# Plain attention on one core: the weighting matmuls between the two score tiles of a period, one period later

## The chip, the cores and the metric

The kernel runs on one core of a Trainium2 chip. The metric is the device time of one execution in microseconds (us), from the first to the last instruction. The engines are TensorE (PE in the profile; PEld is its weight load), VectorE (DVE), ScalarE (ACT), GpSimd (POOL) and SyncE (SP), which issues most DMAs. Each works through its own queue in order, and semaphores order the queues against each other.

## The reference

The input is x with 4 batches of 1024 tokens and 128 dims. Four blocks follow each other, each added to x: a causal attention with rotary keys, a mixture of 8 experts, a plain attention, and the experts again. The change lies in the plain attention:

```python
q = (x @ Wq.T).reshape(N, S, H, hd).transpose(0, 2, 1, 3)     # H = 16 heads of hd = 8
k = (x @ Wk.T)...
v = (x @ Wv.T)...
energy = jnp.einsum('nhqd,nhkd->nhqk', q, k)
attn = jax.nn.softmax(energy / jnp.sqrt(jnp.float32(hd)), axis=3)
out = jnp.einsum('nhql,nhld->nhqd', attn, v)
```

## The kernel before

`attend_plain` (line 1002) works in 16 head stacks (`STEPS`): one batch and 4 heads each. A stack has two halves of 512 query columns, and a half has 16 periods (`NP`). So there are 512 periods t (`LAST`), and all five engines write out the same loop `for t in range(-LEAD, LAST + 8)`.

The kernel computes the scores twice. First, 26 periods ahead (`LEAD`), with queries in rows: `score(w, r)` (line 1081), w = t + 26, fills one half of a double bank `wide[w % 2]` with 128 queries x 512 keys of one head. Two such, with r = 1 and r = 0, make one tile of 1024 columns, and VectorE takes the maximum of each half in one reduction (line 1174). Both `score` matmuls of w go into the bank that reduction w - 2 has read: in front of `score(w, 1)` TensorE waits for it (`s_sf`), and the reduction waits for both scores (`s_s`). The maxima of a half are split by GpSimd in three bf16 parts, turned by a matmul (line 1156), copied by ScalarE (line 1220) and brought by four DMAs into extra rows of the query stack.

Then, in period t, with keys in rows: `t_score(u)` (line 1074) for the units u = 2t and 2t + 1 fills `bank[u % 2]` with 128 keys x 512 queries, from which the maximum is already subtracted through the extra rows. ScalarE takes the exponential into a slot of the ring `pT` (line 1208). In front of `t_score(u)` TensorE waits until exponential u - 2 has read the bank. Four units, one for each head, make a quad; `weigh(quad, half)` (line 1088) multiplies the four exponentials by the values `vst`, for one half of the columns. It issues four matmuls, in the trace eight of 256 columns, into the accumulating bank 2 + J of the half J. One such half of a quad is done in each period.

`t_score(u)` with even u uses the array's rows from 0 and stands beside `score(w, 1)` in the rows from 64; `t_score(u + 1)` with `score(w, 0)` is the other way about. These are called the first and the second pair below. TensorE's order in one period before the change is: first pair, second pair, `weigh` of period t - 2, at the end of a half the transposes, and in one period of 16 the turning of the maxima.

At the end of a half, in periods given by `ends_half(t, later)`: ScalarE copies the weighted sums out (`o_sb`, line 1214), TensorE transposes them in four matmuls (line 1149), VectorE divides by the sum of the exponentials (lines 1188 and 1191), and every second time GpSimd writes the values of the stack after next (line 1247). `late_step` and `step_at` give periods in which steps of the next stage's routing are worked in: a few in stacks 9 to 14, and one in two of three periods behind `BEGIN`, where no scores are left to compute (26 periods).

Of the kernel before, what the change touches and what calls it, by code (L numbers as in the profile page):

```python
# [20 lines left out]
GH = 4  # L21
# [22 lines left out]
def mk_program(nc, x_in, w_kv_down, w_k_up, w_v_up, w_q, w_q_rope, w_k_rope, w_o, wq_b, wk_b, wv_b,  # L44
               router_w, w1, b1, w2, b2, cos2, sin2, out):
    ctx = ExitStack()
    with ctx:
# [954 lines left out]
        def attend_plain(stacks, results, s_parts):  # L1002
# [2 lines left out]
            LAST = 2 * STEPS * NP  # L1005
            HEADS = (0, 2, 1, 3)
            KROW = MROW + 3
            NPB = 2 * GH
            s_row = [sem(f"max_rows{i}") for i in range(2)]
            s_s, s_sf = sem("score_pair", False), sem("score_max", False)  # L1010
            s_mall, s_mch, s_m3, s_mt, s_m = sem("max_whole"), sem("split_chain"), sem("max_split"), sem("max_turned"), sem("max_kept")
# [25 lines left out]
            def half_of(t):  # L1037
                return t // NP
# [28 lines left out]
            def late_step(t, place):  # L1067

                return t >= BEGIN and (t - BEGIN) % 3 == place

            with nc.Block() as block:
                @block.tensor
                def _(e):
                    def t_score(u):
                        s, J, kc, j = unit(u)
                        r, jj, at = j // 2, j % 2, s % NBUF
                        e.matmul(bank[u % 2][:, :], k_st[at][64 * r:64 * r + KROW, jj, kc * P:(kc + 1) * P],  # L1077
                                 q_st[at][64 * r:64 * r + KROW, jj, J * HALF:(J + 1) * HALF],
                                 start=True, stop=True, tile_position=(64 * r, 0)).then_inc(s_st, 1)

                    def score(w, r):
                        s, G, pair, c, kh = score_at(w)
                        at, q0 = s % NBUF, (G % 2) * HALF + c * P
                        e.matmul(wide[w % 2][:, r * HALF:(r + 1) * HALF], q_st[at][64 * r:64 * r + MROW, pair, q0:q0 + P],  # L1084
                                 k_st[at][64 * r:64 * r + MROW, pair, kh * HALF:(kh + 1) * HALF],
                                 start=True, stop=True, tile_position=(64 * r, 0)).then_inc(s_s, 1)

                    def weigh(quad, half):
                        for i in range(GH):
                            u = quad * GH + i  # L1090
                            s, J, kc, j = unit(u)
                            qs = slice(half * HALF // 2, (half + 1) * HALF // 2)
                            ins = e.matmul(bank[2 + J][32 * j:32 * (j + 1), qs], vst[s % 2][:, kc, j, :], pT[:, u % NPB, qs],  # L1093
                                           start=(kc == 0 and half == 0), stop=(kc == NC - 1 and half == 1),
                                           tile_position=(0, 32 * j), skip_group_check=True)
                            if half:
                                ins.then_inc(s_pv, 1)

                    steps = routed.tensor(e)
                    for t in range(-LEAD, LAST + 8):  # L1100
                        w, u = t + LEAD, 2 * t
                        tiles, scores = 0 <= t < LAST, w < LAST
                        if t - 3 in step_at:
                            s = (t - 3) // (2 * NP)
                            e.wait_ge(s_y, PRIME + 2 * s)
                            e.wait_ge(s_m, PRIME + 2 * s + 2)
                            next(steps)
                        if t == BEGIN:
                            e.wait_ge(s_sf, LAST)
                        if late_step(t, 0):  # L1110
                            next(steps, None)
                        if tiles:
                            if t % (2 * NP) == 0:
                                e.wait_ge(stacks.s_in[unit(u)[0] % NBUF], stacks.loaded(unit(u)[0]))
                            if t % NP == 0:
                                e.wait_ge(s_row[half_of(t) % 2], PRIME + (half_of(t) // 2 + 1) * 64)
                            if u >= 2:
                                e.wait_ge(s_p, PRIME + u - 1)
                            t_score(u)
                        if scores:  # L1120
                            if w % (2 * NP) == 0:
                                e.wait_ge(stacks.s_in[score_at(w)[0] % NBUF], stacks.loaded(score_at(w)[0]))
                            if w >= 2:
                                e.wait_ge(s_sf, w - 1)
                            score(w, 1)
                        if late_step(t, 1):
                            next(steps, None)
                        if tiles:
                            if u >= 2:
                                e.wait_ge(s_p, PRIME + u)  # L1130
                            t_score(u + 1)
                        if scores:
                            score(w, 0)
                        if 0 <= t - 2 < LAST:
                            quad, half = divmod(t - 2, 2)
                            if t == 2:
                                e.wait_ge(s_vz, PRIME + 4)
                            if (t - 2) % (2 * NP) == 0:
                                e.wait_ge(s_vs, PRIME + half_of(t - 2) // 2 + 1)
                            if (t - 2) % (2 * NP) == NP and half_of(t - 2) // 2 in LENT:  # L1140
                                e.wait_ge(s_lent, half_of(t - 2) // 2 - LENT[0] + 1)
                            if half == 0:
                                e.wait_ge(s_p, PRIME + (quad + 1) * GH)
                            weigh(quad, half)
                        H = ends_half(t, 3)
                        if H is not None:
                            e.wait_ge(s_oev, PRIME + H + 1)
                            for c in range(CPH):
                                ins = e.transpose(bank[2 + H % 2][:, c * P:(c + 1) * P], o_sb[:, c * P:(c + 1) * P], ident[:, :])
                            ins.then_inc(s_ot, 1)  # L1150
                        G = turns_max(t)
                        if G is not None:
                            e.wait_ge(s_m3, PRIME + G + 1)
                            if G >= 2:
                                e.wait_ge(s_y, PRIME + G - 1)
                            e.matmul(bank[2 + G % 2][0:GH * 3 * CPH, 0:P], mx3[G % 2][:, :, :, :].rearrange("p j i c -> p (j i c)"),
                                     identb[:, :], start=True, stop=True).then_inc(s_mt, 1)
                    drain(steps)

                @block.vector  # L1160
                def _(e):
                    steps = routed.vector(e)
                    for t in range(-LEAD, LAST + 8):
# [7 lines left out]
                        if w < LAST:  # L1171
# [4 lines left out]
                            if w % NP == NP - 1:  # L1176
                                e.wait_ge(s_sf, w + 1)
                                if G >= 2:
                                    e.wait_ge(s_m3, PRIME + G - 1)
                                e.tensor_tensor(mxw[G % 2][:, :, :], mx[G % 2][:, 0, :, :], mx[G % 2][:, 1, :, :],  # L1180
                                                ALU.max).then_inc(s_mall, 1)
                        H = ends_half(t, 4)
                        if H is not None:
                            e.wait_ge(s_ot, PRIME + H + 1)
                            if H >= 1:
# [13 lines left out]
                @block.scalar  # L1199
                def _(e):  # L1200
                    steps = routed.scalar(e)
                    for t in range(-LEAD, LAST + 8):
                        if 0 <= t < LAST:
                            for u in (2 * t, 2 * t + 1):
                                e.wait_ge(s_st, PRIME + u + 1)
                                if u >= NPB:
                                    e.wait_ge(s_pv, PRIME + (u // GH - 1) * GH)
                                e.activation(pT[:, u % NPB, :], bank[u % 2][:, :], ACT.Exp, scale=scale).then_inc(s_p, 1)  # L1208
                        H = ends_half(t, 1)
                        if H is not None:  # L1210
                            e.wait_ge(s_pv, PRIME + (H + 1) * NP * 2)
                            if H >= 1:
                                e.wait_ge(s_ot, PRIME + H)
                            e.activation(o_sb[:, :], bank[2 + H % 2][:, :], ACT.Copy).then_inc(s_oev, 1)
                        G = turns_max(t)
                        if G is not None:
                            e.wait_ge(s_mt, PRIME + G + 1)
                            if G >= 2:
                                e.wait_ge(s_row[G % 2], PRIME + G // 2 * 64)
                            e.activation(nmp[G % 2][:, :], bank[2 + G % 2][0:GH * 3 * CPH, 0:P], ACT.Copy).then_inc(s_m, 1)  # L1220
                        if t - 3 in step_at:
                            next(steps)

                @block.gpsimd
                def _(e):
# [10 lines left out]
                    for t in range(-LEAD, LAST + 8):  # L1236
# [3 lines left out]
                            next(sums, None)  # L1240
                        if t in (19 * NP + 10, 19 * NP + 12):
                            next(normed)
                        H = ends_half(t, 3)
                        if H is not None and H % 2 and H // 2 + 2 < STEPS:
                            s = H // 2 + 2
                            e.wait_ge(s_pv, PRIME + (H + 1) * NP * 2)
# [883 lines left out]
```

## Time and profile before

| | before |
| --- | --- |
| median of 3 runs (lowest, highest) | 2027.02 us (2025.97, 2036.19) |
| profiled execution, own time | 2027.0 us |
| its span | 2027.0 us |
| PE busy | 1782.4 us, 88% |
| DVE busy | 1410.1 us, 70% |
| ACT busy | 1161.5 us, 57% |
| POOL busy | 581.1 us, 29% |

The plain attention of the change takes the time from about 1034 us (first `score`) to 1763 us. Busy shares are means over all stages; the share of a stage is read from windows. A line of a timeline gives start, duration, engine, line, operation, and how many instructions it merges. The duration of a matmul is from its start until its result is there; matmuls overlap, so distances between starts say what TensorE needs.

### The profile page before, as it was taken

What the parts mean: (1) busy time and instruction counts of PE and PEld (TensorE: products, weight loads), DVE (VectorE), ACT (ScalarE), POOL (GpSimd) and SP (SyncE); (2) the same over time, 40 slices, a digit from 0 to 9 for tenths busy, and PEclk for the clock granted to TensorE, in tenths of its full rate; (3) what the DMA queues carried; (4) which work ended last, traced back from release to release, by engine and by line L of the source; (5) the groups of instructions that cost most, each with busy time, mean ns of one, the idle gap of its engine ahead of it and who ended that gap; (6) DMA issues with size and microseconds to landing.
All of it is one profiled execution on the core that took longest, in us unless ns stands there. A gap on an engine that the chain in (4) does not pass through costs nothing. (4 is left out here: it accounts for less than half of the span.)

```text
span 2027.0 us, 40740 instructions
## 1 busy us (share of the span) xinstructions
PE 1782.4 (88%) x15061; PEld 903.7 (45%) x15061; DVE 1410.1 (70%) x3172; ACT 1161.5 (57%) x2314; POOL 581.1 (29%) x817
## 2 busy tenths in 40 slices
PE   5699999999999968799659999999999999777895
PEld 2356666565655545475312222222233332255563
DVE  6676666667788455532669999999899998557431
ACT  3336666666655632232328888888888887332231
POOL 2312122121122146676330000002310000157774
PEclk9779999999999978888769999999999998579798
DMA  5642744553541053232220000000000000062324
GB/s 158 160 81 51 125 84 72 101 90 61 104 81 17 23 143 60 41 53 35 88 110 14 21 17 18 23 27 18 17 18 20 28 5 22 14 168 37 60 38 83
DMA packets 108006, 120.95 MB, mean 60 GB/s; under 512 B 14361, under 2 KB 72961, under 8 KB 107809
## 3 DMA queue, kind: packets, MB, share of 16 engines
q1 hardware_dynamic: 83616, 100.97, 21.1%
q0 software_dynamic: 24192, 17.38, 6.1%
q8 instruction: 120, 1.97, 0.4%
q14 instruction: 78, 0.63, 0.1%
HBM read 81.71 MB, written 35.65 MB: 58 GB/s over the span
## 5 line engine op out<-in xcount | busy, mean ns | idle before, releaser
L1174 DVE TENSOR_REDUCE mx<-wide 128x2 f32<-128x1024 f32 x512 | 604.6, 1220 | 55.2 <-PE wide L1084 42.9
L1208 ACT ACTIVATE pT<-bank 128x512 f32<-128x512 f32 x1024 | 556.8, 596 | 110.9 <-PE bank L1077 102.7
L870 ACT ACTIVATE pT<-bank 128x512 f32<-128x512 f32 (+3 forms) x768 | 350.5, 490 | 248.3 <-PE bank L723 230.0
L1077 PE MATMUL bank<-q_st,k_st 51*128 51x512 bf16 x1024 | 360.4, 397 | 21.0 <-ACT pT L1208 5.2
L1084 PE MATMUL wide<-k_st,q_st 48*128 48x512 bf16 x1024 | 352.6, 399 | 23.6 <-DVE mx L1174 13.9
L1093 PE MATMUL bank<-pT,vst 128*32 128x256 f32 x4096 | 340.2, 405 | 1.8 <-DVEq L1168 1.8
L837 DVE TENSOR_REDUCE mx<-wide 128x1 f32<-128x640 f32 (+3 forms) x256 | 257.2, 1021 | 102.8 <-PE wide L733 97.8
L733 PE MATMUL wide<-k_st,q_st 120*128 120x512 f32 (+3 forms) x768 | 311.1, 417 | 3.5 <-DVE mx L837 1.7
L723 PE MATMUL bank<-q_st,k_st 122*128 122x512 f32 (+3 forms) x768 | 297.8, 392 | 5.5 <-ACT pT L870 3.4
L1793 POOL DMA_INDIRECT acc_rows<-yg,idx x128 | 201.9, 1577 | 105.0 <-DVE yg L2060 71.8
L1077 PEld LDWEIGHTS bank<-q_st,k_st 51*128 51x128 bf16 x1024 | 90.3, 93 | 311.5 <-ACT pT L1208 268.0
L910 POOL TENSOR_SCALAR_AFFINE_SELECT pT<-pT 128x512 f32<-128x512 f32 x128 | 81.0, 633 | 363.8 <-ACT pT L870 363.7
L723 PEld LDWEIGHTS bank<-q_st,k_st 122*128 122x128 f32 x768 | 143.9, 189 | 92.3 <-ACT pT L870 41.6
L1881 PE MATMUL wide<-xgT,w1b 128*128 128x512 f32 x256 | 158.9, 764 | 12.1 <-ACT xgT L1944 4.4
L748 PE MATMUL bank<-pT,vst 128*32 128x256 f32 (+3 forms) x3072 | 164.6, 332 | 1.1 <-POOL pT L910 0.6
L733 PEld LDWEIGHTS wide<-k_st,q_st 120*128 120x128 f32 x768 | 158.9, 208 | 10.7 <-DVE mx L837 9.7
L1093 PEld LDWEIGHTS bank<-pT,vst 128*32 128x32 f32 x4096 | 82.0, 109 | 137.7 <-issue 135.2
L1950 ACT ACTIVATE hT<-wide,b1t 128x512 f32<-128x512 f32 x128 | 87.3, 687 | 95.5 <-PE wide L1881 88.0
L1781 POOL DMA_INDIRECT xg<-xn_rows,idx x128 | 124.7, 974 | 56.6 <-issue 41.8
L731 PE MATMUL wide<-mask_qk,identb 128*128 128x128 bf16 x512 | 121.9, 238 | 16.7 <-PEq L371 11.7
L1255 POOL CAST mx<-mxw 128x16 bf16<-128x16 f32 x32 | 6.3, 196 | 435.2 <-DVE mxw L1180 431.9
L1944 ACT ACTIVATE xgT<-bank 128x512 f32<-128x512 f32 x32 | 19.1, 597 | 163.7 <-PE bank L1869 122.3
(328 smaller groups left out, 2041.0 us busy)
## 6 DMA issues: line engine op xcount, KB each, us to landing
q_st<-rope_split SPq DMA_DIRECT2D x60, 256.0 KB
k_st<-rope_split SPq DMA_DIRECT2D x60, 256.0 KB
qk_split<-parts SPq DMA_DIRECT2D x8, 1024.0 KB, 6.6
q_st<-qk_split SPq DMA_DIRECT2D x96, 64.0 KB
k_st<-qk_split SPq DMA_DIRECT2D x96, 64.0 KB
qk_parts<-parts SPq DMA_DIRECT2D x8, 768.0 KB, 4.6
xn_rows<-xn SPq DMA_DIRECT2D x8, 512.0 KB, 4.0
w1b<-in_L_ffn_w SPq DMA_DIRECT2D x16, 256.0 KB, 5.2
```

Source lines behind the costliest of these rows:

```text
L723: e.matmul(bank[u % 2][:, q0:HALF], k_st[at][0:KROW, j, kc * P:(kc + 1) * P], q_st[at][0:KROW, J, j, q0:HALF], start=True, stop=True).then ...
L733: return e.matmul(wide[w % 2][:, col:col + width], q_st[at][0:KS, G % 2, j, c * P:(c + 1) * P], k_st[at][0:KS, j, kh * HALF:kh * HALF + wi ...
L748: ins = e.matmul(bank[2 + J][32 * j:32 * (j + 1), qs], vst[s % 2][:, kc, j, :], pT[:, u % NPB, qs], start=(kc == 0 and half == 0), stop=(k ...
L837: ins = e.tensor_reduce(mx[G % 2][:, at:at + 1], wide[w % 2][:, 0:HALF + right], AX.X, ALU.max)
L870: e.activation(pT[:, u % NPB, q0:HALF], bank[u % 2][:, q0:HALF], ACT.Exp, scale=scale).then_inc(s_p, 1)
L1077: e.matmul(bank[u % 2][:, :], k_st[at][64 * r:64 * r + KROW, jj, kc * P:(kc + 1) * P], q_st[at][64 * r:64 * r + KROW, jj, J * HALF:(J + 1) ...
L1084: e.matmul(wide[w % 2][:, r * HALF:(r + 1) * HALF], q_st[at][64 * r:64 * r + MROW, pair, q0:q0 + P], k_st[at][64 * r:64 * r + MROW, pair, ...
L1093: ins = e.matmul(bank[2 + J][32 * j:32 * (j + 1), qs], vst[s % 2][:, kc, j, :], pT[:, u % NPB, qs], start=(kc == 0 and half == 0), stop=(k ...
L1174: e.tensor_reduce(mx[G % 2][:, kh, pair:GH:2, c], wide[w % 2][:, :].rearrange("p (r k) -> p r k", r=2), AX.X, ALU.max).then_inc(s_sf, 1)
L1208: e.activation(pT[:, u % NPB, :], bank[u % 2][:, :], ACT.Exp, scale=scale).then_inc(s_p, 1)
L1793: e.indirect_dma_start(acc_dram[n // NE], bass.IndirectOffsetOnAxis(ap=idx[n % 4][:, m:m + 1], axis=0), yg[n % 2][:, m, :], None, compute_ ...
L1881: e.matmul(tile_bank[(tiles_to(n) + k) % 2], w1b[:, ex, k * P:(k + 1) * P], xgT[n % 2][:, :], start=True, stop=True).then_inc(s_h, 1)
```

## The change

`weigh` moves from behind the second pair to between the first and the second pair of a period, and works on period t - 3 in place of t - 2, with all of its waits. The steps that follow the end of a half (copy, transposes, division, values) come one period later with it. The ring of exponentials grows from 8 to 12 slots, and the wait in front of an exponential is written for a ring of any multiple of 4.

```diff
--- before.py
+++ after.py
@@ -1005,7 +1005,7 @@
             LAST = 2 * STEPS * NP
             HEADS = (0, 2, 1, 3)
             KROW = MROW + 3
-            NPB = 2 * GH
+            NPB = 12
             s_row = [sem(f"max_rows{i}") for i in range(2)]
             s_s, s_sf = sem("score_pair", False), sem("score_max", False)
             s_mall, s_mch, s_m3, s_mt, s_m = sem("max_whole"), sem("split_chain"), sem("max_split"), sem("max_turned"), sem("max_kept")
@@ -1123,6 +1123,17 @@
                             if w >= 2:
                                 e.wait_ge(s_sf, w - 1)
                             score(w, 1)
+                        if 0 <= t - 3 < LAST:
+                            quad, half = divmod(t - 3, 2)
+                            if t == 3:
+                                e.wait_ge(s_vz, PRIME + 4)
+                            if (t - 3) % (2 * NP) == 0:
+                                e.wait_ge(s_vs, PRIME + half_of(t - 3) // 2 + 1)
+                            if (t - 3) % (2 * NP) == NP and half_of(t - 3) // 2 in LENT:
+                                e.wait_ge(s_lent, half_of(t - 3) // 2 - LENT[0] + 1)
+                            if half == 0:
+                                e.wait_ge(s_p, PRIME + (quad + 1) * GH)
+                            weigh(quad, half)
                         if late_step(t, 1):
                             next(steps, None)
                         if tiles:
@@ -1131,18 +1142,7 @@
                             t_score(u + 1)
                         if scores:
                             score(w, 0)
-                        if 0 <= t - 2 < LAST:
-                            quad, half = divmod(t - 2, 2)
-                            if t == 2:
-                                e.wait_ge(s_vz, PRIME + 4)
-                            if (t - 2) % (2 * NP) == 0:
-                                e.wait_ge(s_vs, PRIME + half_of(t - 2) // 2 + 1)
-                            if (t - 2) % (2 * NP) == NP and half_of(t - 2) // 2 in LENT:
-                                e.wait_ge(s_lent, half_of(t - 2) // 2 - LENT[0] + 1)
-                            if half == 0:
-                                e.wait_ge(s_p, PRIME + (quad + 1) * GH)
-                            weigh(quad, half)
-                        H = ends_half(t, 3)
+                        H = ends_half(t, 4)
                         if H is not None:
                             e.wait_ge(s_oev, PRIME + H + 1)
                             for c in range(CPH):
@@ -1179,7 +1179,7 @@
                                     e.wait_ge(s_m3, PRIME + G - 1)
                                 e.tensor_tensor(mxw[G % 2][:, :, :], mx[G % 2][:, 0, :, :], mx[G % 2][:, 1, :, :],
                                                 ALU.max).then_inc(s_mall, 1)
-                        H = ends_half(t, 4)
+                        H = ends_half(t, 5)
                         if H is not None:
                             e.wait_ge(s_ot, PRIME + H + 1)
                             if H >= 1:
@@ -1204,9 +1204,9 @@
                             for u in (2 * t, 2 * t + 1):
                                 e.wait_ge(s_st, PRIME + u + 1)
                                 if u >= NPB:
-                                    e.wait_ge(s_pv, PRIME + (u // GH - 1) * GH)
+                                    e.wait_ge(s_pv, PRIME + ((u - NPB) // GH + 1) * GH)
                                 e.activation(pT[:, u % NPB, :], bank[u % 2][:, :], ACT.Exp, scale=scale).then_inc(s_p, 1)
-                        H = ends_half(t, 1)
+                        H = ends_half(t, 2)
                         if H is not None:
                             e.wait_ge(s_pv, PRIME + (H + 1) * NP * 2)
                             if H >= 1:
@@ -1240,7 +1240,7 @@
                             next(sums, None)
                         if t in (19 * NP + 10, 19 * NP + 12):
                             next(normed)
-                        H = ends_half(t, 3)
+                        H = ends_half(t, 4)
                         if H is not None and H % 2 and H // 2 + 2 < STEPS:
                             s = H // 2 + 2
                             e.wait_ge(s_pv, PRIME + (H + 1) * NP * 2)
```

## Rows read from the trace of the kernel before

**Rows 1.** Page, costliest groups: busy us, mean ns of one | idle before, releaser.

```profile
L1174 DVE TENSOR_REDUCE mx<-wide 128x2 f32<-128x1024 f32 x512 | 604.6, 1220 | 55.2 <-PE wide L1084 42.9
L1208 ACT ACTIVATE pT<-bank 128x512 f32<-128x512 f32 x1024 | 556.8, 596 | 110.9 <-PE bank L1077 102.7
...
L1077 PE MATMUL bank<-q_st,k_st 51*128 51x512 bf16 x1024 | 360.4, 397 | 21.0 <-ACT pT L1208 5.2
...
L1093 PE MATMUL bank<-pT,vst 128*32 128x256 f32 x4096 | 340.2, 405 | 1.8 <-DVEq L1168 1.8
```

**Rows 2.** Waits from 1080 to 1450 us: total us, times, longest.

```profile
PEld bank L1077 <- ACT pT L1208: 151.8, 380, 0.7
...
ACT pT L1208 <- PE bank L1077: 39.1, 108, 0.9
DVE mx L1174 <- PE wide L1084: 15.3, 36, 0.5
```

**Rows 3.** Timeline of ScalarE: start us, us, engine, line.

```profile
1186.31 2.19 ACT L1208 ACTIVATE pT<-bank 128x512 f32<-128x512 f32 x4 [0.26 <-PE bank L1077]
1188.77 2.19 ACT L1208 ACTIVATE pT<-bank 128x512 f32<-128x512 f32 x4 [0.26 <-PE bank L1077]
```

**Rows 4.** Timeline of TensorE, two periods.

```profile
1188.34 0.39 PE L1077 MATMUL bank<-q_st,k_st 51*128 51x512 bf16 x1
...
1188.57 0.38 PE L1077 MATMUL bank<-q_st,k_st 51*128 51x512 bf16 x1
...
1188.88 0.64 PE L1093 MATMUL bank<-pT,vst 128*32 128x256 f32 x8
...
1189.45 0.39 PE L1077 MATMUL bank<-q_st,k_st 51*128 51x512 bf16 x1
...
1189.91 0.39 PE L1077 MATMUL bank<-q_st,k_st 51*128 51x512 bf16 x1
...
1190.22 0.64 PE L1093 MATMUL bank<-pT,vst 128*32 128x256 f32 x8
...
1190.80 0.39 PE L1077 MATMUL bank<-q_st,k_st 51*128 51x512 bf16 x1
```

**Rows 5.** Timeline while only scores run (before period 0).

```profile
1039.92 2.34 DVE L1174 TENSOR_REDUCE mx<-wide 128x2 f32<-128x1024 f32 x2
...
1041.19 0.11 PEld L1084 LDWEIGHTS wide<-k_st,q_st 48*128 48x128 bf16 x2 [1.03 <-DVE mx L1174]
```

**Rows 6.** Timeline at the end of a half.

```profile
1192.64 0.39 PE L1084 MATMUL wide<-k_st,q_st 48*128 48x512 bf16 x1
...
1193.10 1.23 DVE L1174 TENSOR_REDUCE mx<-wide 128x2 f32<-128x1024 f32 x1 [0.38 <-PE wide L1084]
...
1193.53 0.66 PE L1149 MATMUL bank<-ident,o_sb 128*128 128x128 f32 x4
1194.11 0.09 PEld L1077 LDWEIGHTS bank<-q_st,k_st 51*128 51x128 bf16 x1 [0.17 <-issue]
...
1194.80 1.23 DVE L1174 TENSOR_REDUCE mx<-wide 128x2 f32<-128x1024 f32 x1 [0.47 <-PE wide L1084]
...
1196.43 1.22 DVE L1174 TENSOR_REDUCE mx<-wide 128x2 f32<-128x1024 f32 x1
```

**Rows 7.** Timeline of ScalarE, copies at ends of halves.

```profile
1128.99 0.60 ACT L1214 ACTIVATE o_sb<-bank 128x512 f32<-128x512 f32 x1
...
1201.76 0.27 ACT L1220 ACTIVATE nmp<-bank 48x128 bf16<-48x128 f32 x1
...
1232.36 0.60 ACT L1214 ACTIVATE o_sb<-bank 128x512 f32<-128x512 f32 x1
```

**Rows 8.** Windows: busy us (instructions) of each engine, PEclk, DMA share, GB/s.

```profile
1300.00:1450.00 150.00, 145.18 (x1434) 43.92 (x1432) 140.65 (x139) 131.42 (x248) 36.13 (x80) 1.00 0.07 23
...
1706.00:1760.00 54.00, 49.93 (x302) 13.01 (x301) 30.00 (x193) 29.84 (x54) 0.83 (x4) 0.53 0.07 21
```

**Rows 9.** Timeline behind the last tile of scores.

```profile
1757.95 0.58 PE L1676 MATMUL wide<-tail,same_rowf 128*128 128x1 f32 x2 [1.07 <-DVE tail L1622]
```

## What was predicted, before the change was run

> **What bounds the kernel now.** I read the page first, then its costliest groups, then the waits of one quiet stretch, then the timeline of single periods. The groups show the change's stage: 512 periods, each with two exponentials of 596 ns on ScalarE, one maximum reduction of 1220 ns on VectorE, two pairs of score matmuls and eight weighting matmuls on TensorE [rows 1]. No engine alone fills a period. In 370 us VectorE waited 15.3 us for the score pairs, ScalarE 39.1 us for TensorE, and TensorE 151.8 us (380 waits) for ScalarE, as prefetched weight loads see it [rows 2]. So the bound is a ring between TensorE and ScalarE, and the timeline shows it: ScalarE does four exponentials in 2.19 us, then waits 0.26 us for a score, again and again, 2.46 us from one group to the next, which is 1.23 us a period [rows 3].
>
> The two periods behind that [rows 4]: pair 1188.34, pair 1188.57, weighting 1188.88; pair 1189.45, pair 1189.91 (0.46 later, held by an exponential), weighting 1190.22, pair 1190.80. I read off the distances between starts that TensorE needs by itself: pair to pair 0.22 (0.23), pair to weighting 0.32, weighting to pair 0.57. With nothing to wait for a period would be 0.22 + 0.32 + 0.57 = 1.11 us. The late exponential every second period makes it 1.23.
>
> VectorE has the third loop. Reduction w and the scores of w + 2 share a double bank, so `score(w+2, 1)` waits for reduction w, and reduction w + 2 waits for `score(w+2, 0)`. Its links: from the start of a reduction to the matmul pair it releases, 1039.92 to 1041.19, 1.27 us [rows 5]; from the start of the second score to its reduction, 1192.64 to 1193.10, 0.46 us [rows 6]. Before the change the two scores lie 0.22 apart, so the loop needs 1.27 + 0.22 + 0.46 = 1.95 us for two periods that take 2.46: half a microsecond of play, and it does not bind.
>
> **The change, part by part.**
>
> Moving the weighting between the pairs. It removes and adds no TensorE instruction. The distances stay too: pair, weighting, pair, next pair is 0.32 + 0.57 + 0.22 = 1.11 us. For the bank that an exponential frees nothing changes either: score tiles of the exponentials were 0.22 and 0.89 apart by turns, now 0.89 and 0.22. I therefore expect no gain for ScalarE. But `score(w, 1)` stands ahead of the eight matmuls and `score(w, 0)` behind them: queued behind the first score's wait for VectorE are the weighting, the next tile of scores and then the very score that this reduction needs. The VectorE loop becomes 1.27 + 0.89 + 0.46 = 2.62 us for two periods, 1.31 us each. That exceeds 1.23: the cover of half a microsecond is gone and VectorE's loop sets the time. Sixteen periods (one half of a head stack): 16 x 1.31 = 20.96 us.
>
> Work at the ends of halves. Before, a whole half takes 20.67 us: the o_sb copies at 1128.99 and 1232.36 are five halves apart [rows 7]. Sixteen times 1.23 is 19.7, so 1.0 us per half is now the work at its ends. In the new order each such item eats the play beside the loop first. VectorE's two normalising operations push one reduction from 1.12 behind the last (2.34 for two, less 1.22 for one) [rows 5] to 1.63 (1194.80 to 1196.43) [rows 6]: 0.51, less the play of 1.31 - 1.12 = 0.19, leaves 0.32. The four transposes now follow the second pair: 0.32 to them and 0.58 from them to the next pair (1193.53 to 1194.11) [rows 6] in place of 0.22, so 0.68 added, less the play of 0.20 (1.31 - 1.11), leaves 0.48. On ScalarE the second exponential of a period now starts late (0.89 + 0.43 after the first pair; 0.43 is from 1188.34 to 1188.77 [rows 3, 4]), ends its slot of 0.53 at 1.85, and the next, ended at 2.45, is needed at 2.62: play 0.17. The 0.60 us copy (a slot of 0.5) [rows 7] leaves 0.32, the 0.27 us copy of the turned maxima (a slot of 0.3) 0.13. All four: 1.25 us. Each falls on one of two interleaved chains, which absorb a little of each other's delays, so I take 1.2 with 0 and 1.4 as ends. A half: 20.96 + 1.2 = 22.2 us, 1.5 more than now.
>
> How often. Scores run 26 periods ahead, so score pairs and tiles run together in 486 of 512 periods: 30.4 halves x 1.5 = 45.6 us. The 26 periods without scores have no VectorE loop. There TensorE runs at 0.50 to 0.53 of full clock and is 49.9 of 54 us busy, with the next stage's routing steps in between [rows 8]; the order of work inside them costs the same either way, between -2 and +2 us. The first half's stretch at low clock is TensorE's own work and counts in the same bound.
>
> A TensorE rule. Pair to pair takes 0.22 us but pair to weighting 0.32 [rows 4], so changing kind of matmul costs about 0.10. A period has two such changes before and after. At a half's end the transposes and the turning of the maxima stood between weighting and pair and now stand between two pairs, one more change for each. The Trainium skill, TensorEngine Tiling (Array Packing), Key Properties, says that changing the tiling mode drains TensorE; by it the edit costs two more drains per half, which the trace prices at about 0.1 us each, some 6 us in all if nothing covered them. By a view that modes are free, they would be nothing. The sums above hold the transposes' own from rows.
>
> One period later, and the tail. Weighting half a quad at t - 3 leaves one more weighting block behind the last score tile. At half the clock a block takes up to twice its 0.57 us. But the routing matmul there waits 1.07 us for VectorE [rows 9], and the additional block falls ahead of it: between 0 and +1 us, I take 0. The o_sb copy, transposes, division and reload of v each move by one period with it; the wait of ScalarE for the last weighting gets shorter, as the weighting is now done mid-period. SP's queue is left where it is. The values for the next stack are needed a period later and are made a period later. From -1 to +1, taken as 0.
>
> The ring of 12. An exponential waits for the weighting of the quad it overwrites. No row of waits has ScalarE on the weighting line for it before [rows 2], and now exponentials of period t overwrite what was weighted by period t - 2. Price 0. With the old ring of 8 the first exponential of every second period would wait for the weighting in the middle of its own period, at 0.32 + 0.57 behind the pair instead of 0.43 [rows 4]; the longer ring is what the move needs. Nothing is gained by it alone.
>
> Sum: 2027.0 + 45.6 = 2072.6 us. The profiled execution's own time is its span, 2027.0, against a median of 2027.02, so nothing is converted.
>
> **Rivals.**
>
> Faster by even spacing. The weighting between the tiles could feed ScalarE evenly and close its 0.26 us gap. For: ScalarE's slot pair is 1.06 us, TensorE's floor 1.11 [rows 3, 4]. Against: the VectorE loop must come under 2.46 us, and it needs scores within 0.73 of each other, where the rows give 0.89. It decides where the weighting between row-tiled pairs costs 0.16 us less than beside them. With a period at 1.18 it gives 16 x 0.05 = 0.8 us a half, 2027 - 24 = 2003 us. Chance 0.05.
>
> No difference. The loop rises only to about 2.5 us, or half-end work disappears wholly in the play: 20.96 against 20.67 is +0.3 a half, +9 us, 2036; with the loop at 2.5, -5 to +5. Chance 0.10.
>
> The clock falls. TensorE's real waiting grows from 0.12 to 0.20 us in each period. In the quiet stretch the granted clock is 1.00 with TensorE 145 of 150 us busy, in the tail 0.53 [rows 8]. The Trainium skill, TensorE: Matmul & The Clock Gate, A second HAM failure mode, tells of a kernel that cycles PSUM banks and idles briefly between matmul groups until its clock oscillates. As a mechanism here: all of TensorE's 1.11 us doubles at half the clock, so a period takes 2.2 us in place of 1.39. If a tenth of the 627 us ran so, some 37 us come on top (63 x (2.2 - 1.39) / 1.39): about 2110. The trace speaks against it, since gaps of ScalarE's kind never lowered the clock there. Chance 0.04.
>
> The change isn't what it says: the order could be moved while waits make it idle. Only the ring is such a part, and it is priced at nothing already.
>
> **How the numbers follow.** Forecast 2073, chance 0.81, own range 2050 to 2090: the low end has loop links 0.04 shorter (16 x 0.02 x 30.4 = 10 us) and half of the half-end work covered, the high end 1.4 of it and links 0.04 longer. With no difference 0.10, faster 0.05, clock 0.04 this fills 1. For eight in ten 2045 to 2092. A change under 0.5% (10 us) is what a measurement of this kernel can't tell. From the cases: faster 0.05, same 0.10, slower 0.85.
>
> **What would show it.** Right: VectorE waiting for the score matmuls in nearly every period, its reductions 1.31 us apart in quiet stretches; weight loads of L1084 released by the reduction, which the rows of waits do not have now; the o_sb copies 22.2 us apart; ScalarE waiting on L1077 as often; weighting starts 0.32 behind a pair. Wrong: the second score under 0.8 us behind the first, reductions 1.23 apart, or a granted clock under 0.95 between 1100 and 1450 us.

## The result: 2.7% slower, by VectorE's loop

| | before | after |
| --- | --- | --- |
| median | 2026.7 us (4 runs) | 2084.6 us (2081.0 to 2089.7, 4 runs) |
| ratio of after to before | | 1.0273, interval 1.024 to 1.0307 |
| profiled execution, own time | 2027.0 us | 2081.0 us |
| its span | 2027.0 us | 2079.1 us |
| plain attention, first reduction to first division of the last half | 1034.3 to 1762.4 us | 1030.1 to 1810.05 us |

The prediction was 2073 us. Placed beside the kernel before once more, on what by its times is another chip (2005.8 us for the kernel before), the kernel after gave 1.0248 (1.0213 to 1.0283). In the profiles the attention takes 51.8 us more and the span 52.1, so the change sits where it was expected. The stages that it doesn't touch moved a little and cancel: the attention starts 4.2 us earlier, and what follows it takes 4.45 us more. The distance between the medians is 4 us larger than between the two profiled executions (54). The slowest of the four executions after (2089.7 us) has the lowest mean granted clock, 0.912 against 0.917 to 0.919; beyond that I can't place these 4 us.

The page's groups after the change. Read the last column: the idle time before an operation, and who ended it.

```profile
L1174 DVE TENSOR_REDUCE mx<-wide 128x2 f32<-128x1024 f32 x512 | 606.6, 1221 | 105.2 <-PE wide L1084 104.7
L1208 ACT ACTIVATE pT<-bank 128x512 f32<-128x512 f32 x1024 | 568.3, 596 | 166.0 <-PE bank L1077 157.2
...
L1077 PE MATMUL bank<-q_st,k_st 51*128 51x512 bf16 x1024 | 363.0, 399 | 26.8 <-ACT pT L1208 17.8
L1093 PE MATMUL bank<-pT,vst 128*32 128x256 f32 x4096 | 342.4, 408 | 0.0
```

The work is what it was [rows 1]: the same counts and the same durations. Waiting has grown on VectorE (55 to 105 us) and on ScalarE (111 to 166 us). The waits from 1080 to 1450 us, in the order total, times, longest:

```profile
PEld bank L1077 <- ACT pT L1208: 138.1, 331, 0.8
...
ACT pT L1208 <- PE bank L1077: 65.4, 168, 0.8
...
DVE mx L1174 <- PE wide L1084: 46.1, 133, 0.6
...
PEld wide L1084 <- DVE mx L1174: 12.6, 16, 0.8
```

VectorE waits for its score matmuls 133 times instead of 36 [rows 2], about once in two periods, and a new row has come: score matmuls held by the reduction. Its 16 waits are one a half, 0.79 us each, where VectorE does other work; in quiet periods the hold is too short for this row. There it shows inside the first pair, whose two matmuls start 0.18 us apart (1188.08 and 1188.26 below) and were 0.01 apart before. Now one turn of the loop, from the timeline of VectorE and TensorE:

```profile
1186.97 2.36 DVE L1174 TENSOR_REDUCE mx<-wide 128x2 f32<-128x1024 f32 x2 [0.27 <-PE wide L1084]
...
1188.08 0.39 PE L1077 MATMUL bank<-q_st,k_st 51*128 51x512 bf16 x1
...
1188.26 0.39 PE L1084 MATMUL wide<-k_st,q_st 48*128 48x512 bf16 x1
...
1188.57 0.64 PE L1093 MATMUL bank<-pT,vst 128*32 128x256 f32 x8
...
1189.15 0.39 PE L1084 MATMUL wide<-k_st,q_st 48*128 48x512 bf16 x1
...
1189.60 2.36 DVE L1174 TENSOR_REDUCE mx<-wide 128x2 f32<-128x1024 f32 x2 [0.27 <-PE wide L1084]
```

A reduction starts at 1186.97. The first score into its bank starts at 1188.26, 1.29 later, when the reduction is over. The weighting comes next, and the second score 0.89 behind the first. The next reduction into the bank starts 0.45 behind that, at 1189.60. Sum 2.63 us for two periods; predicted were 1.27 + 0.89 + 0.46 = 2.62. Reductions come in close pairs and then wait 0.27, since two banks make two interleaved chains.

ScalarE's copies at the ends of halves, two in a row:

```profile
1130.89 0.59 ACT L1214 ACTIVATE o_sb<-bank 128x512 f32<-128x512 f32 x1
...
1153.24 0.59 ACT L1214 ACTIVATE o_sb<-bank 128x512 f32<-128x512 f32 x1
```

A quiet half takes 22.35 us, against 20.67 [rows 7]. Last the end of a half:

```profile
1197.45 0.60 ACT L1208 ACTIVATE pT<-bank 128x512 f32<-128x512 f32 x1 [0.41 <-PE bank L1077]
...
1197.95 0.59 ACT L1214 ACTIVATE o_sb<-bank 128x512 f32<-128x512 f32 x1
...
1199.09 0.39 PE L1077 MATMUL bank<-q_st,k_st 51*128 51x512 bf16 x1 [0.53 <-ACT pT L1208]
...
1199.98 0.39 PE L1084 MATMUL wide<-k_st,q_st 48*128 48x512 bf16 x1
1200.30 0.66 PE L1149 MATMUL bank<-ident,o_sb 128*128 128x128 f32 x4
...
1200.43 1.23 DVE L1174 TENSOR_REDUCE mx<-wide 128x2 f32<-128x1024 f32 x1 [0.58 <-PE wide L1084]
1200.88 0.39 PE L1077 MATMUL bank<-q_st,k_st 51*128 51x512 bf16 x1
...
1202.23 1.23 DVE L1174 TENSOR_REDUCE mx<-wide 128x2 f32<-128x1024 f32 x1 [0.57 <-PE wide L1084]
```

The copy holds exponentials up, and they hold the pair at 1199.09 by 0.53. The transposes stand 0.32 behind the second pair and 0.58 ahead of the next, as the terms of the sum had it, and the two reductions behind wait 0.58 and 0.57 instead of 0.27. What VectorE does next was not all in the sum:

```profile
1203.49 0.17 DVE L1180 TENSOR_TENSOR mxw<-mx 128x16 f32<-128x16 f32 x1
1203.59 0.25 DVE L1188 RECIPROCAL rsum<-bank 128x16 f32<-128x16 f32 x1
1203.87 0.29 DVE L1191 TENSOR_TENSOR v_all<-bank,rsum 128x128 f32<-128x128 f32 x1
1204.08 2.35 DVE L1174 TENSOR_REDUCE mx<-wide 128x2 f32<-128x1024 f32 x2
1206.69 2.36 DVE L1174 TENSOR_REDUCE mx<-wide 128x2 f32<-128x1024 f32 x2 [0.27 <-PE wide L1084]
```

The two normalising operations come one period later than before, and there they meet L1180, which merges the maxima of the half. The reduction starts 1.85 us behind the last one, 0.73 above VectorE's 1.12. From 1206.69 on five turns of 2.63 us follow to the end of the half. The windows of a quiet stretch and of the 54 us behind the last early scores:

```profile
1300.00:1450.00 150.00, 142.19 (x1328) 47.27 (x1327) 130.56 (x129) 121.89 (x229) 21.11 (x52) 1.00 0.05 18
1752.80:1806.80 54.00, 51.23 (x302) 13.42 (x305) 30.90 (x195) 30.43 (x55) 0.83 (x4) 0.55 0.07 21
```

Against [rows 8]: 129 VectorE instructions instead of 139 in 150 us, at full clock both times, and behind the last scores the same 302 matmuls in the same 54 us. From the last reduction to the first division of the last half it is 56.8 us before and 57.2 after.

### The profile page after: what moved, and what is told of

Read it like the earlier page. It is cut to its first block and busy times, and to the rows that moved or that the text cites. A ratio compares the mean times of both kernels' runs of the same rounds, so it can differ in the third digit from the quotient of the medians.

```text
span 2079.1 us, 40736 instructions
## 1 busy us (share of the span) xinstructions
PE 1822.9 (88%) x15061; PEld 932.6 (45%) x15061; DVE 1414.4 (68%) x3172; ACT 1163.2 (56%) x2314; POOL 580.5 (28%) x817
## 3 DMA queue, kind: packets, MB, share of 16 engines
q1 hardware_dynamic: 83616, 100.97, 20.7%
## 5 line engine op out<-in xcount | busy, mean ns | idle before, releaser
L1174 DVE TENSOR_REDUCE mx<-wide 128x2 f32<-128x1024 f32 x512 | 606.6, 1221 | 105.2 <-PE wide L1084 104.7
L1208 ACT ACTIVATE pT<-bank 128x512 f32<-128x512 f32 x1024 | 568.3, 596 | 166.0 <-PE bank L1077 157.2
L1084 PE MATMUL wide<-k_st,q_st 48*128 48x512 bf16 x1024 | 365.8, 402 | 33.4 <-DVE mx L1174 23.7
L1077 PE MATMUL bank<-q_st,k_st 51*128 51x512 bf16 x1024 | 363.0, 399 | 26.8 <-ACT pT L1208 17.8
L1077 PEld LDWEIGHTS bank<-q_st,k_st 51*128 51x128 bf16 x1024 | 89.0, 93 | 313.7 <-ACT pT L1208 262.9
L1084 PEld LDWEIGHTS wide<-k_st,q_st 48*128 48x128 bf16 x1024 | 92.0, 93 | 83.3 <-DVE mx L1174 49.9
```

The lines of the kernel that those rows point to most:

```text
L1174: e.tensor_reduce(mx[G % 2][:, kh, pair:GH:2, c], wide[w % 2][:, :].rearrange("p (r k) -> p r k", r=2), AX.X, ALU.max).then_inc(s_sf, 1)
```

## The experiments

Each was timed beside the kernel before on the same chip, but they were spread over three chips: e1 to e4 on one (median of the kernel before 2005.1 us), e5 to e8 on a second (2000.7), e9 and the second timing of after on a third (2005.8). So ratios are compared, and the length of a quiet half, which repeats to about 0.01 us within a profile. Whole times scatter more than the halves, by up to 1.3% between executions of the same kernel, and e6 was timed only twice.

```
kernel                                   ratio to before (interval)    quiet half, us
before                                   1                             20.67
after                                    1.0248 (1.0213 to 1.0283)     22.35
e1 weighting behind the pairs, t - 3     0.9979 (0.9946 to 1.0011)     20.53
e2 after, scores side by side            1.0066 (1.0035 to 1.0098)     20.98
e3 before, scores parted                 1.0217 (1.0151 to 1.0283)     22.01
e4 after, reductions an eighth shorter   1.0119 (1.0037 to 1.0201)     21.47
e5 after, reductions of half the keys    1.0066 (1.0044 to 1.0087)     20.95
e6 after, ring of 8                      1.0642 (1.0606 to 1.0678)     24.52
e7 e2, transposes behind the weighting   1.0050 (1.0031 to 1.0068)     21.12
e8 e1, transposes a period later         0.9962 (0.9941 to 0.9983)     20.51
e9 before, transposes a period later     0.9957 (0.9936 to 0.9977)     20.45
```

(The half of before is from the chip of the result; the half of after is 22.35 there and in the second timing.)

**Is it the later period or the longer ring?** e1 is the kernel after with one block moved back:

```diff
                         if scores:
                             ...
                             score(w, 1)
-                        if 0 <= t - 3 < LAST:
-                            ...
-                            weigh(quad, half)
 ...
                             score(w, 0)
+                        if 0 <= t - 3 < LAST:
+                            ...
+                            weigh(quad, half)
                         H = ends_half(t, 4)
```

> The kernel after with the weighting put back behind the second pair, but still on period t - 3, with the ring of 12 and the end of a half one period later. Theory (VectorE's loop: the second score stands behind the weighting): the two scores are 0.22 us apart again, the loop is 1.95 us for two periods and does not bind; halves of 20.7 us, the whole 2027 us within 5. Rival depth (the later period and the longer ring cost something at the ends of halves): 2040 to 2080 us.

Ratio 0.9979, halves of 20.53 us, a little under what was expected. The later period and the ring cost nothing; the whole loss is in the block's place.

**What about its place? The two scores, or the two tiles of the exponentials?** Both are parted by the moved block. e2 keeps the weighting between the pairs and brings the two scores of a tile together again, in the second pair of one period and the first of the next:

```diff
-                        if scores:
-                            ...
-                            if w >= 2:
-                                e.wait_ge(s_sf, w - 1)
-                            score(w, 1)
+                        if 1 <= w <= LAST:
+                            score(w - 1, 1)
                         ...
                         if scores:
+                            ...
+                            if w >= 2:
+                                e.wait_ge(s_sf, w - 1)
                             score(w, 0)
```

> The kernel after, weighting still between the two pairs, but tile w of the early scores takes its first half from the second pair of a period and its other half from the first pair of the next, so its two matmuls are 0.22 us apart with no weighting between them. Theory (VectorE's loop): the loop is 1.27 + 0.22 + 0.46 = 1.95 us for two periods, TensorE and ScalarE bound again at 1.23 us a period, halves of 20.7 to 21.0 us, the whole 2027 to 2037 us. Rival ScalarE (the weighting between the tiles u and u + 1 delays the second exponential): as slow as the kernel after, 2075 to 2085 us, halves of 22.3. Rival more changes of the matmul kind: also near 2080.

e3 makes the same edit in the kernel before. There the weighting is behind the second pair, so this edit is what puts it between the two scores.

> The kernel before with the same shift of the scores alone: first half of tile w in the second pair of a period, other half in the first pair of the next, with the weighting of the old order (behind the second pair, t - 2, ring of 8) now between them. No other edit. Theory (VectorE's loop): the two scores are 0.57 + 0.32 = 0.89 us apart, the loop is 2.62 us, 1.31 us a period, halves of about 22.2 us, the whole 2065 to 2085 us. Rivals ScalarE, depth and kinds of matmul: nothing of theirs is changed, 2027 us within 5.

The two are mirror images. e2 has the weighting between the tiles and falls to 20.98 us and 1.0066; the half is in the range expected, the whole just above it (0.66%, where up to 0.5% was expected). e3 has no weighting between the tiles, no later period and no longer ring, and rises to 22.01 us and 1.0217, where about 22.2 was expected. In e2 ScalarE is back in its old rhythm in quiet periods, four exponentials and a wait of 0.26, starts 2.46 apart:

```profile
1188.09 2.19 ACT L1208 ACTIVATE pT<-bank 128x512 f32<-128x512 f32 x4 [0.29 <-PE bank L1077]
1190.55 2.20 ACT L1208 ACTIVATE pT<-bank 128x512 f32<-128x512 f32 x4 [0.26 <-PE bank L1077]
```

In e3 VectorE has the new one, pairs of reductions 2.63 apart, the same distance as in the kernel after:

```profile
1250.00 2.41 DVE L1174 TENSOR_REDUCE mx<-wide 128x2 f32<-128x1024 f32 x2 [0.22 <-PE wide L1084]
1252.63 2.41 DVE L1174 TENSOR_REDUCE mx<-wide 128x2 f32<-128x1024 f32 x2 [0.22 <-PE wide L1084]
1255.26 1.23 DVE L1174 TENSOR_REDUCE mx<-wide 128x2 f32<-128x1024 f32 x1 [0.22 <-PE wide L1084]
```

Of the 1.82 us a half between e1 and after, 1.37 go with the parted scores (22.35 to 20.98). The other 0.45 stay in e2, with the weighting between the tiles. The starts of the tiles say where: the first six periods of a half, with copy and transposes, take 8.26 us in e1 and 8.56 in e2, the other ten, with the turning of the maxima, 12.27 and 12.42. What holds the tiles there was not tested.

**Is the reduction's length in the loop?** If so, a shorter reduction must give its time back twice in two chains, until another loop binds.

```diff
-                                e.tensor_reduce(mx[...], wide[w % 2][:, :].rearrange("p (r k) -> p r k", r=2),
+                                e.tensor_reduce(mx[...], wide[w % 2][:, :].rearrange("p (r k) -> p r k", r=2)[:, :, 0:448],
```

> The kernel after with reductions over 448 of each 512 keys: the maxima leave out an eighth of the keys. A reduction gets about 0.13 us shorter. Theory (VectorE's loop): the loop falls from 2.63 to about 2.50 us for two periods, a half by 8 x 0.13 = 1.0 us, the whole by 30 us to about 2053. Rivals ScalarE and kinds of matmul: VectorE has slack and a shorter reduction gives nothing, 2080 us within 5.

The reduction went from 1221 to 1091 ns, 0.13 us, and pairs of them start 2.50 us apart:

```profile
1183.47 2.26 DVE L1174 TENSOR_REDUCE mx<-wide 128x2 f32<-128x896 f32 x2 [0.24 <-PE wide L1084]
1185.97 2.26 DVE L1174 TENSOR_REDUCE mx<-wide 128x2 f32<-128x896 f32 x2 [0.24 <-PE wide L1084]
```

The loop shrank by exactly the reduction's 0.13. The half fell by 0.88 us where eight turns of it would give 1.04; the five quiet turns give theirs in full (0.65), the other three, with the work at the end of a half, 0.2 to 0.3 instead of 0.39. There the reduction is only part of what binds. With half of the keys (`0:256`):

> The kernel after with reductions over 256 of each 512 keys: the maxima leave out half of the keys. A reduction of 1221 ns falls to some 700 (the cut by an eighth took 130 ns, half takes four times that). Theory (VectorE's loop): 2.63 less 0.52 is 2.11 us for two periods, no longer above the 2.46 of TensorE and ScalarE, so the gain stops there: quiet halves of 20.9 to 21.1 us, as where the two scores are side by side with the weighting between the pairs (20.98). Rival (each shortened reduction gives its time in full, 16 x 0.26 us): halves of 18.2 us. Rival (VectorE's length does nothing once an eighth is cut): 21.47.

692 ns a reduction, a half of 20.95 us. VectorE has half a microsecond more in each period, and nothing of it is gained below what e2 gives: the other loop binds. Both ways of opening VectorE's loop end at the same length (20.95 and 20.98), so parting the scores costs nothing beside that loop.

**The ring.** e6 is the kernel after with `NPB = 8`.

> The kernel after with the ring of exponentials back at 8. The first exponential of every second period then overwrites a quad whose weighting stands behind the first pair of the same period, so it starts about 1.0 us behind that pair instead of 0.43. Theory (my step on the ring): the wait shows as ScalarE waiting for the weighting line every second period, and pushes the next first pair; two periods go from 2.63 to about 2.70 us, a half to 22.7 to 23.3, the whole 15 to 30 us above the kernel after. Rival (the wait is covered by VectorE's loop, which has the time): halves of 22.35 us, no change.

A half of 24.52 us, 2.2 more than after; I had expected 0.4 to 0.9. The direction was right, the size wrong. The waits from 1100 to 1450 us have a row that no other kernel has, and two lines of ScalarE's timeline show its rhythm:

```profile
ACT pT L1208 <- PE bank L1093: 55.4, 115, 0.8
```

```profile
1216.98 1.68 ACT L1208 ACTIVATE pT<-bank 128x512 f32<-128x512 f32 x3 [0.36 <-PE bank L1093]
...
1219.91 1.68 ACT L1208 ACTIVATE pT<-bank 128x512 f32<-128x512 f32 x3 [0.36 <-PE bank L1093]
```

I had added the delay to VectorE's loop. But it closes a loop of its own: the exponential frees the bank for the first pair of the next period (0.66), from there to the period behind it 0.32 + 0.57 + 0.23, then 0.31 to the weighting and 0.84 until the exponential that overwrites it, 2.93 us in all. So with this order of work the longer ring is necessary, though it gains nothing by itself.

**The work at the ends of halves.** e7 takes e2 and moves the transposes and the turning of the maxima ahead of the second pair, right behind the weighting.

> The shifted scores with the weighting between the pairs, and now the transposes and the turning of the maxima right behind the weighting, ahead of the second pair, instead of behind the second pair. Theory (kinds of matmul: pair to transposes costs 0.32 where weighting to transposes replaces a weighting-to-pair of 0.57): about 0.1 us less for each of the two, quiet halves of 20.75 to 20.9 us in place of 20.98. Rival (a late second tile of scores costs ScalarE as much as the change of kind saves): 20.98 or more.

A half of 21.12 us, 0.14 worse; the expectation failed, and the rival named the direction. A change of matmul kind is saved at each of the two places. The transposes are not where it loses: ScalarE waits 0.88 us at once there in place of three times 0.3, nearly the same sum, and the first six periods take 8.54 us against 8.56 in e2. The other ten, with the turning of the maxima, take 12.58 against 12.42. The whole doesn't show a loss: 1.0050 against 1.0066, with intervals that overlap.

The 0.14 us by which e1 beats the kernel before asked for a reason. e8 is e1 with the transposes in period 5 of a half, the division in 6:

> The weighting behind the second pair on period t - 3 (ring of 12) with the transposes at period 5 of a half instead of 4 and the division at 6 instead of 5. Theory (TensorE and ScalarE's loop alternates a period of 1.11 us with one of 1.34 that has 0.23 us of waiting): transposes in the period that waits are partly covered, halves of 20.3 to 20.5 us against 20.53, the whole 0 to 7 us under that kernel and 0.2 to 0.6% under the kernel before. Rival (the copy by ScalarE in period 2 has used up the play): 20.5 or up to 20.7.

A half of 20.51 us, 0.02 under e1. That is just outside the range expected and inside the rival's.

e9 is the kernel before with the same two numbers raised by one, and nothing else:

```diff
-                        H = ends_half(t, 3)
+                        H = ends_half(t, 4)
 ...
                             e.wait_ge(s_oev, PRIME + H + 1)
-                        H = ends_half(t, 4)
+                        H = ends_half(t, 5)
 ...
                             e.wait_ge(s_ot, PRIME + H + 1)
```

> The kernel before (weighting behind the second pair, t - 2, ring of 8) with only the transposes at period 4 of a half in place of 3 and the division at 5 in place of 4. Theory (what the later weighting gained, 20.53 against 20.67 us a half, is only the place of the half-end work in the two-period rhythm): quiet halves of 20.50 to 20.55 us here too, the whole 0.1 to 0.4% under the kernel before. Rival (the later weighting itself gained it): 20.67.

```profile
1120.88 0.60 ACT L1214 ACTIVATE o_sb<-bank 128x512 f32<-128x512 f32 x1
...
1141.33 0.60 ACT L1214 ACTIVATE o_sb<-bank 128x512 f32<-128x512 f32 x1
```

20.45 us a half, a little under the range expected, ratio 0.9957. So a gain over the kernel before needs neither the later weighting nor the longer ring. Where it comes from shows in TensorE's order. By turns the second pair starts 0.23 us behind the first, or about 0.45 when an exponential holds it. The turning of the maxima (L1156) stands behind a held pair in the kernel before, and behind a pair that was not held in e1:

```profile
1200.15 0.39 PE L1077 MATMUL bank<-q_st,k_st 51*128 51x512 bf16 x1
...
1200.59 0.39 PE L1077 MATMUL bank<-q_st,k_st 51*128 51x512 bf16 x1
...
1201.48 0.24 PE L1156 MATMUL bank<-identb,mx 128*48 128x128 bf16 x1
```

```profile
1166.33 0.39 PE L1077 MATMUL bank<-q_st,k_st 51*128 51x512 bf16 x1
...
1166.57 0.38 PE L1077 MATMUL bank<-q_st,k_st 51*128 51x512 bf16 x1
...
1167.45 0.24 PE L1156 MATMUL bank<-identb,mx 128*48 128x128 bf16 x1
```

Read the four kernels by the distance inside the pair ahead of the transposes, and of the turning: before 0.49 and 0.44 (a half of 20.67), e1 0.49 and 0.24 (20.53), e8 0.22 and 0.45 (20.51), e9 0.23 and 0.25 (20.45). Each of the two is cheaper behind a pair that was not held, where it takes the place of the next wait. e1 got its 0.14 by the turning, not by the transposes; e8 moved the transposes to the good place and lost it for the turning; e9 has both. This is read from traces, and no run moves the turning alone. e8 and e9 are both about 0.4% faster than the kernel before and can't be told from each other by time; e9 is the smaller edit.

> The kernel after, unchanged, beside the kernel before of the same chip as the other runs. Theory (the loss is the loop and the ends of halves, neither of which depends on the chip): ratio to the kernel before 1.024 to 1.031, quiet halves of 22.35 us. Rival (part of the loss was the other chip's): under 1.024.

1.0248 and 22.35 us: the length of the half is the same as beside the result. The chip is that of e9, not that of e1 to e8, so the ratios of e1 to e8 are set against it across chips.

## Why the prediction was right, step by step

- **The bound before** was read rightly: TensorE and ScalarE alternate 1.11 and 1.34 us, VectorE has slack. e5 shows it from the other side: with VectorE's loop opened wide in the new order, a half does not fall below 20.95.
- **VectorE's loop** was forecast as 2.62 us and measured as 2.63, link by link. It is the step that carries the result, and e2, e3 and e4 each change one link of it and get its share.
- **The half-end work** was taken as 1.2 us; 22.35 - 16 x 1.315 = 1.31 was measured. The trace has it all in three turns, from the reduction at 1197.49 to the one at 1206.69 (9.20 us, where three quiet turns take 7.89). ScalarE's copy costs 0.31 (0.32 in the sum). The transposes and VectorE's own work cost 1.0, where the sum has 0.48 + 0.32. The 0.2 between are L1180, a term that the sum lacks. In the kernel before it adds 0.22 to a reduction's 1.12 too (from 1196.43 in [rows 6] to 1197.77 below). The copy of the turned maxima, 0.13 in the sum, costs nothing, as all turns behind 1206.69 are of 2.63. So one term was left out and one was charged in vain, and the small difference between 1.2 and 1.31 is in part luck.

```profile
1197.68 0.17 DVE L1180 TENSOR_TENSOR mxw<-mx 128x16 f32<-128x16 f32 x1
...
1197.77 2.35 DVE L1174 TENSOR_REDUCE mx<-wide 128x2 f32<-128x1024 f32 x2
```

- **From 2073 to 2084.6.** A half cost 1.68 us more in place of the 1.5 forecast, times 30.4 is 5.5 us. That accounts for all but 0.7 of the step from 45.6 to 51.8 in the profiled attention. The rest up to the medians' 57.9 is 0.3 in the other stages, 1.9 by which the own time of the profiled execution exceeds its span (2081.0 and 2079.1; before the change they were equal), and the 4 us not placed. The range was 2050 to 2090; the low end as it is described adds up to 2045.
- **No cost of the later period, tail unchanged**: right. Shown by e1, and by a tail of 56.8 us before and 57.2 after.
- **No gain or loss for ScalarE by the weighting between its tiles**: right in quiet periods (e2: 2.46 us for two), wrong for a half as a whole, where e2 takes 0.45 us more than e1. With the scores together again, this is what is left of the loss.
- **The ring priced at nothing**: right with 12. With 8 the forecast named the wait, and e6 shows it at 2.2 us a half.
- **Two more changes of matmul kind per half**, about 0.1 us each: pair to transposes is 0.32 in the trace, as expected. The Trainium skill (TensorEngine Tiling (Array Packing), Key Properties) says that a change of tiling mode drains TensorE. e7 saved one such change at each of the two places and its half still got 0.14 longer, so this price isn't what decides here, and no run isolates it.
- **The rivals**: even spacing did not pay (e2 is still not under before). The clock stayed at 1.00 in the quiet stretch though TensorE's busy time there fell from 145.2 to 142.2 of 150 us.
- **The signs**: reductions 1.31 us apart on average, scores 0.89 apart and longer halves came as named. Three did not come as written: VectorE waits in every second period and not in nearly every one, the waits of L1084's weight loads are one a half, and ScalarE waits on L1077 more often than before (168 times against 108), not as often.

## What to carry to other kernels

When work is moved in one engine's order, look for pairs of instructions that one buffer ties together: the first waits for a reader and the last releases it. Whatever is put between the two is added to that reader's loop. With two buffers, as here, a turn of the loop covers two periods: it costs nothing while the turn is shorter than they are (1.95 against 2.46 us), and sets the time once it is longer (2.63). Add the loop's links from distances between starts before building, and list every instruction of the reader's engine that falls between two of its turns; the one that was left out here was worth 0.22 us a half. Here that gave the turn within 0.01 us, and the same edit with the pair kept together costs about a quarter of it.

## What the runs showed that was not expected

- The period in which four transposes and the division behind them are placed is worth 0.2 us of a half of 20.7 (20.45 in e9 against 20.67), about 0.4% of the kernel with what the tail gains. By the traces it counts whether the second pair ahead of such a piece of work was held by an exponential.
- A ring two thirds as long closes a loop of 2.93 us and costs 2.2 us a half, more than the change itself (1.7).
